# Row order (chunk, step) for the token tiles of an adaLN block with a chunked recurrence and a gated FFN

## The reference, cut to what matters

```python
x = L0_attn_x                                     # (8, 1024, 256) float32
mod = (silu(c) @ wmod).reshape(8, 6, 1, 256)      # sa, ca, ga, sb, cb, gb; |ga|, |gb| at least 0.25
h = layernorm(x) * (1 + ca) + sa
xb = einsum('bsd,ed->sbe', h, B)                  # for each of 1024 steps
for t in range(1024): h_t = tanh(h_{t-1} @ A.T + xb_t);  y_t = h_t @ C.T
x = x + ga * (layernorm(y + h) * gamma + beta)
h = layernorm(x) * (1 + cb) + sb                  # again (8, 1024, 256)
for b in range(8):                                # the batch is the scan axis of the FFN's state
    c = sigmoid(h_b wf' + c uf' + bf) * c + sigmoid(h_b wi' + c ui' + bi) * tanh(h_b wc' + c uc' + bc)
x = x + gb * tanh(h wo' + c_final uo' + bo)
```

## Time and profile before

| | us |
|---|---|
| median of 3 runs (559.84 to 561.21) | 560.26 |
| span of the profiled execution | 558.3 |
| PE busy | 542.1 (97%) |
| DVE busy | 394.1 (71%) |
| POOL busy | 344.1 (62%) |
| ACT busy | 341.0 (61%) |

### The profile page before, as it was taken

How to read it: one execution, slowest core, us unless ns; L and a number is a source line. 1 busy time by engine, 2 the same in 40 slices (tenths; PEclk the granted TensorE clock), 3 DMA queues, 4 the chain that set the end, 5 groups by cost and what they waited for, 6 DMA issues and landing times.

```text
span 558.3 us, 13427 instructions
## 1 busy us (share of the span) xinstructions
PE 542.1 (97%) x4620; PEld 531.2 (95%) x4620; DVE 394.1 (71%) x908; ACT 341.0 (61%) x862; POOL 344.1 (62%) x475
## 2 busy tenths in 40 slices
PE   6999999999999999999999999999999999999994
PEld 3899999999999999999999999999999999999983
DVE  5998878886767665555866676776667676686663
ACT  3777777785466555465765556666665566667651
POOL 4767777660376444454776666677666757778454
PEclk9999999999999999999999999999999999999998
DMA  8666445434243222222133333443333333323244
GB/s 274 181 189 197 146 151 152 127 103 154 85 139 108 72 72 75 78 68 77 57 105 103 103 103 94 120 124 107 96 95 96 95 96 103 123 78 114 67 114 153
DMA packets 58514, 64.10 MB, mean 115 GB/s; under 512 B 5408, under 2 KB 49736, under 8 KB 58448
## 3 DMA queue, kind: packets, MB, share of 16 engines
q1 hardware_dynamic: 58448, 63.26, 37.2%
HBM read 46.44 MB, written 16.81 MB: 113 GB/s over the span
## 4 chain that ended last, share of the span: by engine, by line
PE 76%; POOL 7%; issue 6%; ACT 4%; DVE 3%; DMA 2%; SPq 1%; POOLq 0%; DVEq 0%; ACTq 0%
PE psI L1578 11%; PE psOF L1578 11%; PE psG L1578 11%; PE psWR L1537 6%; PE psWR L1636 6%; PE psWR L1449 4%; PE psWR L1484 4%; PE psOF L1484 4%; PE psOF L1449 4%; PE psC L1564 3%; PE psOF L1564 3%; PE psT L1615 2%; POOL wx L705 2%; ACT xn L851 1%; PE psC L1501 1%
## 5 line engine op out<-in xcount | busy, mean ns | idle before, releaser
L649 POOL TENSOR_TENSOR hin<-hin,uvec 128x256 f32<-128x256 f32 x64 | 50.9, 816 | 32.5 <-ACT hin L813 30.1
L656 POOL TENSOR_TENSOR hsl<-hs,hsh 128x512 fp32r<-128x512 f32 x24 | 30.9, 1289 | 49.1 <-DVE state L1304 32.6
L1285 DVE SCALAR_TENSOR_TENSOR lo<-psT,cb1T,hi 128x256 fp32r<-128x256 f32 x60 | 26.2, 478 | 41.8 <-ACT hi L878 41.8
L690 POOL TENSOR_TENSOR zn<-zn,tA 128x512 f32<-128x512 f32 x32 | 46.1, 1440 | 11.0 <-ACT zn L851 11.0
L1150 DVE TENSOR_TENSOR pre<-psWR,state 128x256 f32<-128x256 f32 x44 | 18.5, 420 | 46.1 <-PE psWR L1537 45.8
L851 ACT ACTIVATE zn<-state,nmA,rstdA 128x256 f32<-128x256 f32 x64 | 35.0, 594 | 26.1 <-POOL nmA L680 26.1
L1537 PE MATMUL psWR<-hs,AT 128*128 128x128 f32 x368 | 49.5, 274 | 0.0
L663 POOL TENSOR_TENSOR xin<-xin,tA 128x512 f32<-128x512 f32 x32 | 41.3, 1289 | 13.3 <-DMA tA<-rows_d 13.3
L840 ACT ACTIVATE hs<-pre 128x256 f32<-128x256 f32 x44 | 18.4, 417 | 50.7 <-DVE pre L1150 50.5
L1104 DVE SCALAR_TENSOR_TENSOR hin<-xin,mvA,uvec 128x256 f32<-128x256 f32 x56 | 41.4, 777 | 9.5 <-DMA h_park<-hin 9.0
L1537 PEld LDWEIGHTS psWR<-hs,AT 128*128 128x128 f32 x368 | 45.2, 191 | 0.1
(11 more groups left out here) (384 smaller groups left out, 2313.4 us busy)
## 6 DMA issues: line engine op xcount, KB each, us to landing
h_park<-hin SPq DMA_DIRECT2D x32, 256.0 KB, 2.2
hin<-h_park SPq DMA_DIRECT2D x64, 128.0 KB
xin<-in_L_attn_x_dram SPq DMA_DIRECT2D x64, 128.0 KB
tA<-rows_d SPq DMA_DIRECT2D x32, 256.0 KB, 4.4
out_dram<-state SPq DMA_DIRECT2D x64, 128.0 KB
xin<-in_L_attn_x_dram SPq DMA_DIRECT2D x28, 256.0 KB, 2.8
tW<-rows_d SPq DMA_DIRECT2D x32, 128.0 KB, 3.2
tG<-rows_d SPq DMA_DIRECT2D x24, 128.0 KB, 3.6
```

The source lines that it names most:

```text
L649: pool.tensor_tensor(h, h, sa, ALU.add).then_inc(a_h, 1)
L690: pool.tensor_tensor(two(zn[:, :]), two(zn[:, :]), both(tA[:, m % 2, 0:D]), ALU.mult).then_inc(s_zg, 1)
```

## The change

Within a half tile the rows go in the order (chunk, step) in place of (step, chunk). `x_t`, `out_t` and the parked rows become patterns of 16 x 8 x 256 in DRAM; a parked pair becomes two neighbouring rows of 1 KB for each partition. `hsh` and `hsl` get the step as their innermost dimension, `hs` keeps the chunk there. So ACT's copy and the subtraction on DVE or POOL now walk `hs` as before, in runs of 16 chunks, and `hsh` and `hsl` with a distance of 8 elements (32 bytes) from one element to the next. No instruction is added, removed or moved.

```diff
--- before.py
+++ after.py
@@ -82,11 +82,11 @@
     TANHS = (LAST + 1, LAST + 3, LAST, HELD, LAST + 2, HELD + 1, HELD + 2)
 
     x_v = x.rearrange("b (k t) d -> (b k) (t d)", k=K)
-    x_t = x.rearrange("b (k t) d -> b t k d", k=K)
-    out_t = out.rearrange("b (k t) d -> b t k d", k=K)
+    x_t = x.rearrange("b (k t) d -> b k t d", k=K)
+    out_t = out.rearrange("b (k t) d -> b k t d", k=K)
     wmod_v = wmod.rearrange("(k p) n -> p k n", p=P)
-    h_park = nc.dram_tensor("h_park", [L, P, D], f32, kind="Internal").ap()
-    h_park_t = h_park.rearrange("t (b k) d -> b t k d", b=NB)
+    h_park = nc.dram_tensor("h_park", [P, L, D], f32, kind="Internal").ap()
+    h_park_t = h_park.rearrange("(b k) t d -> b k t d", b=NB)
     rows_d = nc.dram_tensor("rows_d", [NB, 4, D], f32, kind="Internal").ap()
 
     ctx = ExitStack()
@@ -120,8 +120,8 @@
 
 
         state = sb("state", [P, PAIRS * W])
-        hsh = sb("hsh", [P, 2, H, NB, HT, K], f32r)
-        hsl = sb("hsl", [P, 2, H, NB, HT, K], f32r)
+        hsh = sb("hsh", [P, 2, H, NB, K, HT], f32r)
+        hsl = sb("hsl", [P, 2, H, NB, K, HT], f32r)
         hs = sb("hs", [P, H, NB, 4, K])
         hi = sb("hi", [P, 2, H, POS], f32r)
         lo = sb("lo", [P, 2, H, POS], f32r)
@@ -370,7 +370,11 @@
 
         def pair_of(t, first):
 
-            return t[:, :, :, first:first + 2, :].rearrange("p m b t k -> p m b (t k)")
+            return t[:, :, :, first:first + 2, :].rearrange("p m b t k -> p (m b) t k")
+
+        def split_pair(t, first):
+
+            return t[:, :, :, :, first:first + 2].rearrange("p m b k t -> p (m b) t k")
 
         def by_chunk(t):
             return t.rearrange("p (b k) -> p b k", b=NB)
@@ -416,7 +420,7 @@
             if n < NU - 2:
                 return few[:, n % 2, :, :]
             i = (n - NU + 2) * H * POS
-            return state_of[:, 0].rearrange("p m b t k -> p (m b t k)")[:, i:i + H * POS].rearrange("p (k n) -> p k n", k=H)
+            return state_of[:, 0].rearrange("p m b k t -> p (m b k t)")[:, i:i + H * POS].rearrange("p (k n) -> p k n", k=H)
 
         def hi_at(n):
             return split_of(n, hi, hsh)
@@ -495,7 +499,7 @@
                 if has(ref, 2, PAIRS):
                     sp.wait_ge(a_h, v.lin(2, -2))
                     p = pair1(v, ref, 2)
-                    sp.dma_start(h_park[bass.ds(p * 2, 2), :, :].rearrange("t p d -> p t d"),
+                    sp.dma_start(h_park[:, bass.ds(p * 2, 2), :],
                                  two(htok(ref - 2))).then_inc(a_park3[(ref - 2) % 3] if ref - 2 < THREE else a_park[ref % 2], 16)
                 for what in LOADS.get(ref, []):
                     load(what)
@@ -514,14 +518,14 @@
                     sp.wait_ge(s_z, c - 2)
                 for i in range(2):
                     sp.dma_start(hin[:, c % 3, i * D:(i + 1) * D],
-                                 h_park_t[b + i, T * TB + j * HT:T * TB + (j + 1) * HT, :, :]).then_inc(s_h[c % 3], 16)
+                                 h_park_t[b + i, :, T * TB + j * HT:T * TB + (j + 1) * HT, :]).then_inc(s_h[c % 3], 16)
 
             def load_x(m):
                 if m >= 2:
                     sp.wait_ge(s_x1, m - 1)
                 for j in range(2):
                     sp.dma_start(xin[:, m % 2, j * D:(j + 1) * D],
-                                 x_t[m % NB, steps(m, j), :, :]).then_inc(s_x[m % 2], 16)
+                                 x_t[m % NB, :, steps(m, j), :]).then_inc(s_x[m % 2], 16)
                 sp.dma_start(tA[:, m % 2, :],
                              rows_d[m % NB:m % NB + 1, 0:2, :].rearrange("o i d -> o (i d)").broadcast_to([P, W])
                              ).then_inc(s_tA[m % 2], 16)
@@ -555,7 +559,7 @@
                 else:
                     sp.wait_ge(s_fin, LAST + ON_DVE.index(o) + 1)
                 for j in range(2):
-                    sp.dma_start(out_t[o % NB, steps(o, j), :, :],
+                    sp.dma_start(out_t[o % NB, :, steps(o, j), :],
                                  tiles_of(o)[:, j, :]).then_inc(s_out, 16)
 
             def unit2(u):
@@ -611,7 +615,7 @@
                     store(o)
                 for j, done, n in ((0, s_fin, LAST + len(ON_DVE) + 1), (1, s_fp, len(ON_POOL) + 1)):
                     sp.wait_ge(done, n)
-                    sp.dma_start(out_t[(NU - 1) % NB, steps(NU - 1, j), :, :], tiles_of(NU - 1)[:, j, :]).then_inc(s_out, 16)
+                    sp.dma_start(out_t[(NU - 1) % NB, :, steps(NU - 1, j), :], tiles_of(NU - 1)[:, j, :]).then_inc(s_out, 16)
                 clear(of_middle[len(of_middle) // 2:])
 
                 sp.wait_ge(r_over, r * 4 + 4)
@@ -653,7 +657,7 @@
                     pool.wait_ge(s_hsl, AP)
                 pool.wait_ge(s_hsh, p + 1)
                 j, t = p // 4 % 2, p % 4 * 2
-                pool.tensor_tensor(pair_of(hsl[:, j], t), pair_of(hs, 2 * p % 4), pair_of(hsh[:, j], t).bitcast(f32),
+                pool.tensor_tensor(split_pair(hsl[:, j], t), pair_of(hs, 2 * p % 4), split_pair(hsh[:, j], t).bitcast(f32),
                                    ALU.subtract).then_inc(s_hsl, 1)
 
             def xg_of(m):
@@ -844,7 +848,7 @@
                 if p >= 8:
                     act.wait_ge(s_C, projected(p // 8 - 1, p // 4 % 2))
                 j, t = p // 4 % 2, p % 4 * 2
-                act.activation(pair_of(hsh[:, j], t), pair_of(hs, 2 * p % 4), ACT.Copy).then_inc(s_hsh, 1)
+                act.activation(split_pair(hsh[:, j], t), pair_of(hs, 2 * p % 4), ACT.Copy).then_inc(s_hsh, 1)
 
             def normal(dst, m, nm, rstd, done):
                 for j in range(2):
@@ -1131,7 +1135,7 @@
             def low(p):
                 dve.wait_ge(s_hsh, p + 1)
                 j, t = p // 4 % 2, p % 4 * 2
-                dve.tensor_tensor(pair_of(hsl[:, j], t), pair_of(hs, 2 * p % 4), pair_of(hsh[:, j], t).bitcast(f32),
+                dve.tensor_tensor(split_pair(hsl[:, j], t), pair_of(hs, 2 * p % 4), split_pair(hsh[:, j], t).bitcast(f32),
                                   ALU.subtract).then_inc(s_hsl, 1)
 
             def boundary():
@@ -1561,7 +1565,7 @@
                             n += 1
                             if h is hsl and n == 3 and i == 0:
                                 pe.wait_ge(s_hsl, 8 * T + 4 * j + 4)
-                            last = pe.matmul(ps[:, i * D:(i + 1) * D], h[:, j, k, b + i, :, :].rearrange("p t k -> p (t k)"), w["C"][:, k, :],
+                            last = pe.matmul(ps[:, i * D:(i + 1) * D], h[:, j, k, b + i, :, :].rearrange("p k t -> p (k t)"), w["C"][:, k, :],
                                              start=(n == 1 and i == 0), stop=(n == 3 * H), skip_group_check=True)
                 if end == 2:
                     last.then_inc(s_C, 1)
```

## The result

| | before | after |
|---|---|---|
| median of 5 runs, us | 560.26 (559.79 to 561.21) | 563.86 (563.35 to 564.01) |
| ratio, 95% interval | | 1.0065 [1.0054, 1.0076] |
| span of the profiled execution, us | 558.3 | 562.2 |
| PE / DVE / ACT / POOL busy, us | 542.1 / 394.1 / 341.0 / 344.1 | 543.9 / 401.9 / 355.7 / 355.6 |
| DMA packets, of them under 2 KB | 58514, 49736 | 55954, 43080 |

The changed kernel is slower by 3.6 us in the median and 3.9 us in the profiled executions; I had forecast +1.1. Lines of the kernel after are those of before plus 4 (L1134 is L1138 there, L656 is L660, L847 is L851). In the other runs they shift by a few. One of the five runs of lows_behind took 610.6 us at a granted clock of 0.85 in place of 1.00 and is left out of its time.

The account below looks back on a forecast made before the run. PE bounds the kernel (busy 97% of the span): its fixed work, stalls reaching it, and the ends. Stage one +1.7, stage two's start +1.3, tail -1.9 give +1.1 us: 561.4 us median; 8-in-10 range 558.0 to 564.2.

Parts of the forecast that it names:

- DVE in stage one: Units 29 to 32: four longer subtractions before one lo with 0.44 us slack make PE late by 4 x 0.53 - 0.44 = 1.68 us.
- d: Extra time of each strided subtraction on DVE, taken as 512 x 1.04 ns = 0.53 us.
- ACT's e is hidden there: Stage one: ACT's longer copy, 0.4 us extra, costs nothing, since ACT idles 0.65 to 0.7 us a unit and DVE holds PE.
- The mark that I had set for ACT: Sign of being wrong: ACT's copy L847 over 1.1 us, since ACT would then hold the recurrence in stage one.
- The upper end of d: Bound on DVE's extra time per subtraction: 1.03 us, from the slowest subtraction of the same shape, 1711 ns.
- The last lows of stage one: From unit 33 on: no more scalings, DVE idles 1.0 us and more in each unit, so the last subtractions cost nothing.
- no engine waits for a tile load in stage two: Stage two: faster DMAs from the new patterns are worth nothing almost everywhere except at the end.
- POOL where stage two starts: Three longer POOL subtractions in a chain PE waits for: 0.7 us late at tile 1, 1.3 us in all at tile 2.
- f: Extra time of each strided subtraction on POOL, taken as 0.6 us.
- The tail: End of the kernel: stores spread from half to all 16 DMA engines, gaining 1.9 us, range 0 to 2.4.
- the backlog: Last stores: 14 halves drain in 0.70 us each while issues come every 0.65; removing this backlog gains 0.7 us.
- the stores don't spread, or SP's clears hold the end: Rival at the kernel's end: the tail's gain is 0, sum +3.0 us, 563.3 us; chance 0.12.

Follow-up runs that it names:

- lows_behind: The changed kernel with POOL's subtractions low(8), low(9) and low(10) moved out of the chain to xn at stage two's start; 565.81 us (median of four), ratio 1.0093.
- write_only: The changed kernel with hsh written and read as one run, only the write of hsl strided; output not the reference's; 561.09 us in a single execution.
- states_only: The kernel before with the strided states (chunk, step) alone and the old DRAM patterns; output not the reference's; 563.42 us, ratio 1.0058.
- tables_first: The changed kernel with DVE's five small copies for shift_wo (split_tables) moved ahead of low(7), nothing else; 562.53 us, ratio 1.0045.

## Why the prediction was right and wrong

**DVE in stage one: right, +1.65 for +1.7, though by a wrong size.** Place, wait and releaser are as said: DVE without idle, PE late for `lo` in units 30, 31 and 33 (in unit 32 by 0.05 only). But d was 0.43, not 0.53, and 4 x 0.43 - 0.44 is 1.3, near the 1.4 that PE loses at `lo`. Even that is partly luck: the formula holds DVE's scalings at their old length, and they grew by 0.6 us beside POOL, while write_only, with the same d and shorter scalings, loses 0.73. So the step "ACT's e is hidden there" was not quite right either: PE waits once for ACT's `hs` (0.26), and the 0.9 between after and write_only comes with the other strided sides. The mark that I had set for ACT (over 1.1 us it would hold the recurrence) was borne out in unit 32 alone: it takes 1.18, and elsewhere it is DVE that PE waits for. The upper end of d, 1.03 us, was a misread row: the 1711 ns of the earlier trace rows are not a slow instruction but one that waits for POOL. In before 11 of those 28 take 1.68 us or more, and in each of them a POOL instruction had started 0.11 to 0.15 us earlier (timelines of DVE and POOL):

```profile
272.39 1.69 DVE L1251 TENSOR_TENSOR clo<-cst,chi 128x512 fp32r<-128x512 f32 x1
...
272.27 1.26 POOL L685 TENSOR_TENSOR wx<-wx,tG 128x512 f32<-128x512 f32 x1
```

The collision that cost most at the boundary was thus already in the trace of before.

**The last lows of stage one: wrong, +1.6 for 0.** The step that failed is "from unit 33 on DVE idles 1.0 us and more in each unit, and the last lows cost nothing". It weighed idle time, and not the slack of each thing that stands behind: `split_tables` comes right behind `low(7)` and ended 0.9 us ahead of PE's `shift_wo` before (137.26 for 138.15). ACT's copy ahead of `low(7)` became 0.65 longer (1.28 for 0.63) and `low(7)` itself 0.6 (1.30 for 0.69), together more than that. By these lengths alone PE loses some 0.6, as it does in states_only. The greater part is the collision with POOL's addition to `xin`, and it comes from the DMA half: the step "no engine waits for a tile load in stage two" passed over POOL, which waits 13.29 us for `tA` before and starts as soon as it lands. With the tables' slack used up by the states' half, that collision reaches PE in full; tables_first takes it out of PE's way.

**POOL where stage two starts: right in place and sum, +1.1 for +1.3, the sum by luck, since its path for tile 1 was wrong.** f is 0.37, not 0.6. By the formula of the prediction, (2 x 0.37 + 0.13 - 0.62) + 0.37 = 0.6. What made up for it: `low(8)` starts 0.4 later and not 0.1, because ACT's copy costs 0.55, and the delay goes through DVE's copy `h_skip`, which POOL blocks, to `lo`, and not through `xn`.

**The tail: wrong, 0 for -1.9.** That the stores would spread was right (0.77 at 213 GB/s for 0.56 at 199, and 1.00 at 301 with two issuing engines), and the drain behind the last issue is 0.8 us shorter. The term that failed is the backlog: I let the issue chain keep up, while it is the chain that is last: 16 issues with no gap over 0.4 us, from 547.39 to 558.9. It was so before as well (16 issues, from 543.45 to 554.2), and the plateau at 199 GB/s, which I read as the mark of half of the engines, is also the rate of that chain. The chain then grew by 0.8 us, by the one slow issue, and that cancels the shorter drain. The rival "the stores don't spread, or SP's clears hold the end" had the right number, 0, with a wrong reason: they spread, and the issues, not the clears, hold it.

**Nothing in the steady part, nothing for the parked pair: right.** 379.78 us for 379.81.

Together: +1.65 + 1.6 + 1.1 + 0, less 0.4 us before unit 27 that no part of the change explains, is the +3.9 of the profiled executions. The forecast of +1.1 stood at less than a third of that: one term missing of 1.6, one of -1.9 that wasn't there, and the other two right to 0.2. The range holds 563.86, in its upper part, where the case without a gain at the end had put 563.3; that it does is partly luck, for no rival had a term at the boundary.

## What to carry to other kernels

A strided side costs where it stands on each engine in its own way: price the write and the read apart, and for each engine. Before a lengthened instruction is called free because its engine idles behind it, follow each small instruction that stands behind it to its first reader, and look what POOL does at that moment: a copy of 16 columns can cost a microsecond. A slowest row of a kind is worth a look at what stood beside it, before it is taken for a price. A plateau of the DMA engines says nothing by itself: compare it with bytes per issue over the time between issues, and see whether the queue that issues has gaps.

## What the runs showed of the hardware that I had not expected

- 512 columns written at 32 bytes from element to element cost DVE 0.43 us and ACT 0.55 us more, POOL 0.02; read so from one of two sources they cost POOL 0.35 us more, and at 64 bytes 0.59 (ACT 0.12, DVE 0.01).
- A DVE copy or a subtraction with two inputs in SBUF that starts while a POOL subtraction or addition runs mostly ends with it or its own length behind it: 0.18 became 1.20, 0.69 became 2.10, 1.1 became 2.12; and POOL waits likewise (1.29 became 2.08). The same `h_skip` copy took 0.28, 0.88 and 1.57 us in three orders of POOL's work.
- A store of 128 KB takes SP 0.60 to 0.64 us to issue in either pattern of three dimensions, where the table loads take 0.33, and with the new pattern one of the last 16, always the sixth or seventh, takes 1.1 to 1.7 us in all ten traces, with the old one in none of four.
